# Graph layer and slice attention on one core: GpSimd's gathers held to stages of TensorE, and one-hots made in one comparison a burst

## What is computed

```python
x = x + gnn(layernorm(x), edges)          # 1
x = x + ffn(layernorm(x))                 # 2
# gnn
agg   = segment_sum(x[src], dst, 6250)                 # gather rows, add by destination
h     = relu(agg @ W_rel + b_rel + x @ W_root)         # 512 wide
i,f,g,o = split(h @ W_ih.T + b_ih + b_hh, 4)
y     = (sigmoid(o) * tanh(sigmoid(i) * tanh(g))) @ W_fc + b_fc
# ffn: per head (8 heads, 64 slices), over all 6250 rows as one batch
w     = softmax(((x @ W_x + b_x) @ W_slice + b_slice) / temperature)
token = (w.T @ (x @ W_fx + b_fx)) / (w.sum(0) + 1e-5)   # then attention over 64 tokens
out   = (w @ attention(token)) @ W_out + b_out
```

## Time and profile before

| | us |
|---|---|
| median of 3 runs | 1309.71 |
| lowest and highest run | 1306.66, 1309.84 |
| profiled execution, its span | 1305.9 |

### The profile page before, as it was taken

The page is one execution under the profiler, slowest core; times in us unless marked ns, Lnnn a source line. Parts: engine busy times, 40 slices in busy tenths (PEclk is TensorE's granted clock), DMA queues, the critical chain, the costliest instruction groups (busy, mean ns, idle before and its releaser), DMA issues.

```text
span 1305.9 us, 25399 instructions
## 1 busy us (share of the span) xinstructions
PE 1195.5 (92%) x8519; PEld 1062.2 (81%) x8519; DVE 814.4 (62%) x2352; ACT 609.5 (47%) x1225; POOL 841.4 (64%) x883
## 2 busy tenths in 40 slices
PE   1066998999999999999999999999999999999998
PEld 0064887988888888888888888888988888898798
DVE  5662455675667656766666566756675667546665
ACT  4721335454544455444535454545444554455432
POOL 3467777777777777777777777777777777700000
PEclk9986999999999999999999999999999999999999
DMA  7764345445544454445444554455444544423399
GB/s 237 258 211 119 111 125 146 137 115 146 145 137 127 131 145 135 135 122 145 144 129 121 144 145 135 115 145 146 136 119 138 145 136 132 127 67 95 109 333 288
DMA packets 127895, 191.81 MB, mean 147 GB/s; under 512 B 55661, under 2 KB 88403, under 8 KB 127819
## 3 DMA queue, kind: packets, MB, share of 16 engines
q0 software_dynamic: 41008, 111.77, 29.6%
q1 hardware_dynamic: 74852, 57.47, 15.5%
q10 hardware_dynamic: 11979, 21.94, 5.0%
HBM read 159.02 MB, written 32.92 MB: 147 GB/s over the span
## 4 chain that ended last, share of the span: by engine, by line
POOL 45%; PE 28%; issue 16%; ACT 3%; DVE 3%; DMA 3%; SPq 1%; POOLq 0%; DVEq 0%; ACTq 0%
POOL ring L658 45%; PE ps L344 6%; PE ps L346 6%; PE ps L345 6%; PE ps L1019 3%; PE ps L1120 2%; DMA ring<-in_x 1%; DMA table<-ring 1%; ACT ps L782 1%; ACT L764 1%; PE ps L1108 1%; ACT x L772 1%; PE ps L965 1%; ACT ring L721 1%; DVE oneh L1454 0%
## 5 line engine op out<-in xcount | busy, mean ns | idle before, releaser
L658 POOL DMA_INDIRECT ring<-table,sidx x851 | 812.8, 955 | 268.8 <-issue 268.5
L344 PE MATMUL ps<-h_h,wih_h 128*128 128x256 f32 x1200 | 346.2, 289 | 0.0
L345 PE MATMUL ps<-h_l,wih_h 128*128 128x256 f32 x1200 | 339.6, 283 | 0.0
L346 PE MATMUL ps<-h_h,wih_l 128*128 128x256 f32 x1200 | 339.4, 283 | 0.0
L1019 PE MATMUL ps<-ring,oneh 128*125 128x512 f16 x974 | 231.3, 383 | 14.3 <-DMA ring<-table,sidx 14.2
L344 PEld LDWEIGHTS ps<-h_h,wih_h 128*128 128x128 f32 x1200 | 229.7, 191 | 3.5 <-issue 0.4
L345 PEld LDWEIGHTS ps<-h_l,wih_h 128*128 128x128 f32 x1200 | 229.9, 192 | 1.7
L346 PEld LDWEIGHTS ps<-h_h,wih_l 128*128 128x128 f32 x1200 | 229.7, 191 | 0.0
L797 ACT ACTIVATE gate<-ps,bgate 128x256 f32<-128x256 f32 x300 | 125.5, 471 | 205.4 <-PE ps L346 204.4
L1019 PEld LDWEIGHTS ps<-ring,oneh 128*125 128x125 f16 x974 | 132.0, 138 | 82.6 <-DMA ring<-table,sidx 21.7
L1454 DVE TENSOR_SCALAR oneh<-iota,rel 128x125 f16<-128x125 f16 x974 | 166.5, 285 | 1.8
(11 more groups left out here) (227 smaller groups left out, 2504.9 us busy)
## 6 DMA issues: line engine op xcount, KB each, us to landing
ring<-table,sidx POOLq DMA_INDIRECT x851, 2.8
swt_d<-swt ACTq DMA_DIRECT2D x25, 500.0 KB
gate<-swt_d SPq DMA_DIRECT2D x19, 500.0 KB, 5.8
table<-ring SPq DMA_DIRECT2D x11, 512.0 KB, 7.0
xn<-table SPq DMA_DIRECT2D x25, 224.0 KB
xin<-in_x SPq DMA_DIRECT2D x25, 224.0 KB
res<-xin SPq DMA_DIRECT2D x25, 224.0 KB
ring<-in_x SPq DMA_DIRECT2D x9, 512.0 KB, 6.9
```

What stands on the lines that cost most here:

```text
L344: eng.matmul(dst, wh, xh, start=first, stop=False)
L345: eng.matmul(dst, wh, xl, start=False, stop=False)
L346: return eng.matmul(dst, wl, xh, start=False, stop=last)
L658: pool.indirect_dma_start(ring[:, j, :], None, table, bass.IndirectOffsetOnAxis(ap=sidx[:, odd * SLOTS + j:odd * SLOTS + j + 1], axis=0)). ...
```

## The change

`pace(p, n)` is called ahead of every group of gathers. For ten of the twelve groups (all but 0 and 6) it makes GpSimd wait until a semaphore of TensorE has reached a count, which stands for a stage of turn p - 1 (n up to 7) or of turn p (n from 8 on): for n = 1, 3, 4 and 5 the gates of pair p - 2 up to 4, 6, 8 and 10; for 2 the logits of pair p - 3, for 7 the transposes in its token sums; for 8 `transpose_x(p-1)`, for 9 `out_layer(p-2)`, for 10 `graph_layer(p-1)`, for 11 `transpose_x2(p-2)`. Counts of zero or less are left out. In `one_hots` the loop of 18 or 20 comparisons becomes one `tensor_tensor` over [128, n, 125]: `iota` is repeated over the n slots, and each of the n columns of `rel` is repeated over 125 elements. `rel` becomes fp16.

```diff
--- before.py
+++ after.py
@@ -135,7 +135,7 @@
         ident16 = sb("ident16", [P, P], F16)
         iota = sb("iota", [P, P], F16)
         wbase = sb("wbase", [P, NW + 2])
-        rel = sb("rel", [P, 2 * HOTS])
+        rel = sb("rel", [P, 2 * HOTS], F16)
         sidx = sb("sidx", [P, QUAD], I32)
         didx = sb("didx", [P, 2 * HOTS], I32)
         ones = sb("ones", [P, 1])
@@ -672,6 +672,16 @@
                 pool.wait_ge(gen_idx, NG * ROUNDS * 32 + 2 * LIST)
                 pool.sem_inc(gather_go, 1)
 
+            def pace(p, n):
+
+                stage, done = {
+                    1: (gate_mm, MT // 2 * (p - 2) + 2), 2: (lg_mm, 2 * (p - 2)), 3: (gate_mm, MT // 2 * (p - 2) + 3),
+                    4: (gate_mm, MT // 2 * (p - 2) + 4), 5: (gate_mm, MT // 2 * (p - 2) + 5),
+                    7: (swt_mm, 2 * (p - 2)), 8: (xt_done, p), 9: (y_mm, p - 1), 10: (h_mm, 2 * p),
+                    11: (x2t_mm, p - 1)}.get(n, (None, 0))
+                if stage is not None:
+                    after(pool, stage, done)
+
             def gathers(p, odd):
                 for e in range(2):
                     for k, used in enumerate((half_used[e], sum_done[e])):
@@ -679,6 +689,7 @@
                             pool.wait_ge(idx_in[e], LIST * p + LIST)
                         after(pool, used, p)
                         for q in range(3):
+                            pace(p, 6 * e + 3 * k + q)
 
                             if e == 0 and k == 1 and q == (2 if odd else 1):
                                 after(pool, half_used[1], p)
@@ -1450,9 +1461,9 @@
 
                 dve.tensor_scalar(rel[:, first:first + n], didx[:, idx:idx + n], base, None, ALU.subtract).then_inc(rel_sem, 1)
                 dve.wait_ge(rel_sem, rel_n)
-                for j in range(first, first + n):
-                    last = dve.tensor_scalar(oneh[:, j, 0:WN], iota[:, 0:WN], rel[:, j:j + 1], None, ALU.is_equal)
-                last.then_inc(hot_sem, 1)
+                dve.tensor_tensor(oneh[:, first:first + n, 0:WN], iota[:, 0:WN].unsqueeze(1).to_broadcast([P, n, WN]),
+                                  rel[:, first:first + n].unsqueeze(2).to_broadcast([P, n, WN]),
+                                  ALU.is_equal).then_inc(hot_sem, 1)
 
             with dve.If(general):
                 dve.sem_inc(gen_sum, 1)
```

## The result

The changed kernel takes 1420.64 us (median of 4 runs, 1416.79 to 1422.59), the kernel before beside it 1308.85 (4 runs). The ratio is 1.085 [1.0833, 1.0867]: 112 us slower. The forecast was 1411 with a range of 1368 to 1436; the time lies in it, 10 us above the forecast. The profiled execution's span is 1419.5, against 1305.9.

The account below looks back on a forecast made before the run. GpSimd's gathers, 1.25 us each from start to start, were taken as the bound. Gathers held by the comparisons add 101.5 us to the 1305.9 span, giving 1407.4; 3.8 more to the timed median gives 1411 us (range 1368 to 1436).

Parts of the forecast that it names:

- GpSimd is the bound, and passes on each us: Gathers on GpSimd need 1.25 us each, start to start; each us of slowing makes TensorE wait one us more.
- The length of the comparison: On VectorE, one comparison a burst would take 2.79 us for 2500 elements or 2.53 for 2250, mean 2.72.
- The hold, (end - start) - 0.13, one a burst: Each comparison delays one gather until it ends, by its end minus the gather's start minus 0.13 us; 50 bursts.
- the rival of a capped hold: A long VectorE instruction lets the gather in after about 0.25 us: +10.5 us, 1320; chance 0.03.
- no others of over 1.2: Expected sign in the profile: apart from one gather beside each comparison, no gather takes over 1.2 us.
- The phase: Where gathers start against each comparison sets the hold: 2.07 us a burst taken, 103.5 us over 50 bursts.
- kept phases: Gathers beside the bursts keep their earlier timing: 2.18 us held a burst, 109 us in all.
- a: Time from the comparison's start to the next gather's, 0 to 1.25 us; the hold is 2.72 - 0.13 - a.
- What the present bursts cost: Holds of gathers beside the old comparisons, 0.04 us a burst, would go: 2 us off.
- Why today's bursts hold little: Gathers beside the old bursts take 0.96 and 1.02 us, as each piece is short with one SBUF input.
- The holds at stages: GpSimd's 230 waits for TensorE stages never bind, smallest margin 17.1 us: zero cost, at most 12 us.
- The clock: Rival: TensorE's waits lower its granted clock, making turns longer than GpSimd's; 1458 at the most; chance 0.04.

Follow-up runs that it names:

- e5: The changed kernel, but each burst is 18 or 20 two-input comparisons of one slot each: 1430.15 us, 1.092 of the kernel before.
- e7: The changed kernel, but each burst's single comparison has one tensor input, iota against one column of rel: 1324.80 us, 1.012 of the kernel before.
- e2: The changed kernel with the waits on TensorE's stages, but the old loop of comparisons and rel in fp32: 1307.09 us, 1.000 of the kernel before.
- e11: The kernel before plus the waits alone, with group 5's wait moved to transpose_x2(p-2) so that it binds: 1379.82 us, 1.051 of the kernel before.
- e12: The changed kernel with the middle burst ahead of low_x2 and low_x2t: 1621.84 us, the kernel before beside it 1925.59, ratio 0.842.
- e9: The changed kernel, but each burst is 9 or 10 two-input comparisons of two slots each: 1319.45 us, 1.005 of the kernel before.
- e10: The changed kernel, but with single-slot comparisons having two inputs and one tensor input in turn, rel in fp32: 1326.95 us, 1.011 of the kernel before.
- e8: The kernel before plus a one-input tensor_reduce of 18 or 20 repeats of iota ahead of each burst: 1345.21 us, 1.027 of the kernel before.

## Why the prediction was right

**GpSimd is the bound, and passes on each us.** Right. The earlier trace rows give 0.3 us of "issue" before each gather, and the busy share of 64% hides it. The table shows it over 16 to 120 us. The pairs take 46.0 to 48.2 us (the first 49.7, the last 45.6), some 47 were forecast. The last gather starts at 1253.68; 1242 was forecast, low by the terms below.

**The length of the comparison.** Right: 2.77 and 2.50 us, forecast 2.79 and 2.53 by a slope between two other instructions. No credit for the shorter VectorE time: it gave nothing, as said.

**The hold, (end - start) - 0.13, one a burst.** Right in all 50. The trace of before held more for it than I had read: two gathers of the preparation, at 81.02 and 100.33, were already held for 0.48 and 0.67 us, beside two-input instructions of 1.2 us, by the same formula. My sentence that no gather is delayed by more than 0.25 was false, and the rival of a capped hold rested on it. For the same reason "no others of over 1.2" failed twice: two gathers of the preparation take 1.90 and 1.47 in the changed kernel.

**The phase.** This is the term that was mis-sized. I had 2.18 us a burst for kept phases, 1.96 for an even spread, took 2.07 and so 103.5 us; it is 2.20 and 110.1, at a mean a of 0.37. That is +6.6 us. The phase is not spread because GpSimd holds VectorE too. Ahead of each comparison VectorE makes `rel`, by a subtraction of 0.22 to 0.24 us. In 31 of 50 bursts it takes longer, 0.26 to 0.47, and ends within 0.006 us of the end of a gather: in the rows above at 661.31 + 0.31 = 661.62, where the gather ends at 660.48 + 1.14 = 661.62. The comparison starts 0.03 after that and the next gather 0.30, so a is 0.27, whatever the phase was before. In exactly these 31 bursts it is 0.26 to 0.28; in the other 19 it runs from 0.08 to 1.28. The kernel before had it too: the comparison at 608.22 starts 0.03 after the end of the gather from 607.16, and its subtraction ends with that gather:

```profile
607.88 0.31 DVE L1451 TENSOR_SCALAR rel<-didx,wbase 128x20 f32<-128x20 int32 x1
```

**What the present bursts cost.** 2 us were to come off, and they did: gathers beside the old bursts were held for 2.3 us in all. But the holds beside other instructions rose, from 5.4 to 9.9 us (busy time less 851 gathers of 0.946, less those beside the bursts), which the prediction had as unchanged. Together 2.2 us were added. With 1.4 us at the first gather and after the last, the three make 6.6 + 4.2 + 1.4 = 12.2 us, by which the span was low (1407.4 against 1419.5). The time was low by 10 only, and that is luck: 3.8 us were added from the profiled span to the median of the timed runs, and it was 1.1 this time.

**Why today's bursts hold little.** The prediction gave two reasons, that each piece is short and that it has one input from SBUF. Shortness is not one of them: e5 has pieces as short, with two inputs, and loses 120 us. The single input is what counts, but not for every form: the fast one of e7 holds with one.

**The holds at stages.** Right: e2. The smallest margin in the changed kernel is 17.4 us, over 230 waits, and the gap before a group's first gather stays 0.30.

**The clock.** It fell 12 times between 159 and 1173 us, once before, as the rival feared. It cost nothing: the gathers' holds and idle time account for the whole stretch, and no gather waited for a stage of TensorE. As the text behind the rival said, a late TensorE no longer waits. e11 has the clock fall where TensorE is the later of the two.

Leaving out e12, whose runs can't be compared, no version beats the kernel before.

## What to carry to other kernels

Where GpSimd issues indirect transfers one behind the other, multiply the number by start-to-start time, not by busy time, before calling it idle. Then look at what VectorE does beside it: an instruction there with two SBUF inputs can cost GpSimd up to its whole length, so fusing many short one-input instructions into one long two-input instruction can lose although VectorE gets faster. If it must have two inputs, cut it into pieces with seams between them, and measure: of the sizes tried here 0.41 us cost least, and 0.29 was too short. And look at whether a gather holds the VectorE instruction ahead: it can set the phase of what comes next.

## What the runs showed of the hardware that was not expected

- A row of two-input VectorE instructions of 0.286 us, 0.20 us apart, kept a gather that started 1.22 us or more into the row out for the rest of it, up to 2.7 us (e5); pieces of 0.41 us, 0.33 apart, did so for 0.07 in nearly all cases (e9), and with a one-input piece between each two it was 0.24 at the most (e10).
- A comparison with one SBUF tensor and a scalar column over 2500 16-bit elements takes 0.88 us, a third of the 2.77 with a repeated second input, and it holds gathers all the same, for up to 0.5 us (e7). A reduction of 2.76 us over one input held none (e8).
- Gathers that started up to 0.03 us after a VectorE instruction with two SBUF inputs were not held by it, those from 0.035 us on were (both kernels, no exception).
- A gather holds VectorE as well: 31 of 50 subtractions from int32 to fp16 over 20 numbers took 0.26 to 0.47 us in place of 0.23 and ended with a gather, to within 0.006 us.
- TensorE's granted clock was 0.53 of 2.4 GHz over the 11 us that hold its waits of 2.65 and 3.46 us, and 1.00 in the 47 us that followed.
